# One bank for the natural scores and two for the Gram products in the second attention layer

## The reference

```python
scores_t = jnp.einsum('bhsd,bhtd->bhst', q, k_t) * attn_scale
probs_t = jax.nn.softmax(scores_t, axis=-1)
text_out = jnp.einsum('bhst,bhtd->bhsd', probs_t, v_t)
...
attn_scores = jnp.einsum('bhsd,bhnd->bhsn', q, k_ip) * attn_scale
qsem = jnp.einsum('bhst,bte->bhse', probs_t, text_ehs)
qsem = _l2norm(qsem)
ip_n = _l2norm(ip_ehs)
sem = jnp.einsum('bhse,bne->bhsn', qsem, ip_n)
fused = attn_scores + SEM_SCALE * sem
probs_ip = jax.nn.softmax(fused, axis=-1)
probs_ip = probs_ip * spatial_mask[None, None, :, None]
ip_out = jnp.einsum('bhsn,bhnd->bhsd', probs_ip, v_ip)
...
out = text_out + IP_SCALE * ip_out
out = out @ W_out + b_out
out = out + residual
```

## Time and profile before

| | us |
|---|---|
| median of 3 runs | 1635.77 |
| lowest, highest | 1634.82, 1635.92 |
| the profiled execution | 1634.38 |
| its span in the trace | 1632.3 |
| PE busy in the span | 1562.8 (96%) |
| DVE busy | 1393.3 (85%) |
| ACT busy | 1015.1 (62%) |
| POOL busy | 716.2 (44%) |

### The profile page before, as it was taken

One profiled execution on the slowest core, in us unless ns is written; L12 is line 12 of the kernel. 1 busy time (PEld: TensorE's weight loads), 2 busy tenths in 40 slices (PEclk: granted clock), 3 DMA queues, 4 the chain that ended last, 5 costly groups with the idle time before them and its releaser, 6 DMA issues.

```text
span 1632.3 us, 42423 instructions
## 1 busy us (share of the span) xinstructions
PE 1562.8 (96%) x13960; PEld 1385.0 (85%) x13960; DVE 1393.3 (85%) x4083; ACT 1015.1 (62%) x2444; POOL 716.2 (44%) x629
## 2 busy tenths in 40 slices
PE   6999999999999999998999999999999999999986
PEld 5888888888888888787798889988898888888965
DVE  4687787887888888876899999999999999999985
ACT  3455555565565566655667667667666777676652
POOL 3234432223322332433556555655655655555541
PEclk9999999999999999997999999999999999999988
DMA  8334444444444434543334323332333323332211
GB/s 228 99 107 122 121 126 131 119 127 125 123 130 124 124 117 128 142 124 97 90 91 123 101 69 109 104 105 70 106 95 105 95 83 104 108 103 65 82 38 35
DMA packets 204099, 175.29 MB, mean 107 GB/s; under 512 B 45313, under 2 KB 203403, under 8 KB 203883
## 3 DMA queue, kind: packets, MB, share of 16 engines
q1 hardware_dynamic: 203882, 172.59, 36.7%
HBM read 112.12 MB, written 60.38 MB: 106 GB/s over the span
## 4 chain that ended last, share of the span: by engine, by line
PE 87%; DVE 7%; issue 3%; ACT 1%; DMA 1%; SPq 1%; POOL 0%; DVEq 0%; ACTq 0%; POOLq 0%
PE MISC L144 26%; PE GP L144 20%; PE NAT L333 10%; PE TR L347 8%; PE PV L393 5%; PE PV L378 4%; PE PV L375 3%; PE PV L396 2%; PE MISC L293 2%; DVE ZP L957 1%; PE MISC L437 1%; DVE TMP L848 1%; PE MISC L436 1%; PE MISC L312 1%; PE GP L317 1%
## 5 line engine op out<-in xcount | busy, mean ns | idle before, releaser
L1050 POOL TENSOR_TENSOR ZS<-ZP 128x256 f32<-128x256 f32 x267 | 275.2, 1031 | 285.0 <-DVE ZP L957 284.0
L606 ACT ACTIVATE P<-TA 128x512 f32<-128x512 f32 x320 | 202.3, 632 | 279.3 <-DVE TA L945 276.1
L333 PE MATMUL NAT<-KS,QS 65*128 65x256 f32 x1280 | 300.0, 317 | 8.0 <-ACT SC L560 5.5
L967 DVE SCALAR_TENSOR_TENSOR PM<-P,PH 128x512 f32<-128x512 f32 x320 | 275.2, 860 | 0.0
L144 PE MATMUL GP<-PH,GH 128*128 128x256 f32 (+1 forms) x960 | 248.8, 289 | 21.4 <-DVE ZP L957 21.1
L347 PE MATMUL TR<-QS,KS 69*128 69x256 f32 (+2 forms) x1280 | 259.5, 284 | 4.1 <-DMA QS<-max_rows 2.2
L333 PEld LDWEIGHTS NAT<-KS,QS 65*128 65x128 f32 x1280 | 201.6, 192 | 64.4 <-issue 49.8
L852 DVE TENSOR_REDUCE MX<-NAT 128x2 f32<-128x504 f32 x320 | 215.9, 675 | 36.5 <-PE NAT L333 33.0
L144 PE MATMUL GP<-PH,GL 128*128 128x256 f32 (+1 forms) x960 | 242.7, 281 | 0.0
L281 POOL TENSOR_TENSOR PARTS<-QKF,PARTS 112x512 fp32r<-112x512 f32 (+1 forms) x93 | 121.2, 1304 | 276.0 <-ACT PARTS L635 233.4
L609 ACT ACTIVATE P<-TR 128x512 f32<-128x512 f32 x320 | 192.6, 602 | 60.1 <-PE TR L347 59.3
(11 more groups left out here) (264 smaller groups left out, 3784.6 us busy)
## 6 DMA issues: line engine op xcount, KB each, us to landing
QS<-qk_parts SPq DMA_DIRECT2D x480, 64.0 KB
KS<-qk_parts SPq DMA_DIRECT2D x480, 64.0 KB
qk_parts<-PARTS SPq DMA_DIRECT2D x128, 224.0 KB, 2.9
CT<-in_ctx_t SPq DMA_DIRECT2D x32, 512.0 KB, 3.9
qk_parts<-PARTS SPq DMA_DIRECT2D x64, 192.0 KB, 2.4
XT<-in_x_t SPq DMA_DIRECT2D x48, 112.0 KB, 2.7
XT<-x_t SPq DMA_DIRECT2D x48, 112.0 KB, 2.3
XB<-in_x SPq DMA_DIRECT2D x16, 320.0 KB, 4.2
```

Source lines behind the costliest of these rows:

```text
L333: ins = e.matmul(NAT[s % 2][:, i * T:(i + 1) * T], QS[0:KQ, h, i * 128:(i + 1) * 128], KS[0:KQ, h, :], start=True, stop=True)
L606: e.activation(P[:, s % NP, :], TA[:, s % 2, :], ACT.Exp, scale=SCALE).then_inc(q["exp"], 1)
L967: e.scalar_tensor_tensor(PM[:, s % 2, :], P[:, (S1 + s) % NP, :], 2.0, PH[:, s % NS, :].bitcast(F32), ALU.mult, ALU.subtract).then_inc(q[" ...
L1050: e.tensor_tensor(ZS[s % NZ][:, :], ZP[:, s % 2, 0:S], ZP[:, s % 2, S:2 * S], ALU.add).then_inc(q["zs"], 1)
```

## The change

Layer 1's natural scores all go to NAT[0]; NAT[1] becomes a second bank for the Gram products, which alternate between the old GP bank (even heads) and NAT[1] (odd heads). The waits follow: NAT waits for MX and SC of the head just before instead of two before, GP waits for ZP of two heads before instead of one (and head 1 for the last maximum of layer 0, which is the last reader of NAT[1]). PH gets one more wait, for PM of four heads before. Layer 0 keeps its two NAT banks. No instruction that computes is added or removed.

```diff
--- before.py
+++ after.py
@@ -221,7 +221,14 @@
     TR = [bank(f"TR{k}") for k in range(2)]
     PV = bank("PV")
     ring = Ring([bank(f"MISC{k}") for k in range(2)] + [bank("GP")])
-    GP = ring.banks[2]
+
+    def nat_bank(s):
+
+        return NAT[s % 2 if s < S1 else 0]
+
+    def gp_bank(s):
+
+        return (ring.banks[2], NAT[1])[s % 2]
 
     def take(key, freed, t, slots=None):
 
@@ -325,12 +332,14 @@
                     e.wait_ge(q["clear_q"], 1)
                 if h % HG == 0:
                     e.wait_ge(q[f"stack{h // HG}"], stacked(b + 1))
-                if s >= 2:
+                if s >= S1:
+                    e.wait_ge(q["mx"], s)
+                elif s >= 2:
                     e.wait_ge(q["mx"], s - 1)
-                if s >= S1 + 2:
-                    e.wait_ge(q["sc"], s - S1 - 1)
+                if s > S1:
+                    e.wait_ge(q["sc"], s - S1)
                 for i in range(2):
-                    ins = e.matmul(NAT[s % 2][:, i * T:(i + 1) * T], QS[0:KQ, h, i * 128:(i + 1) * 128],
+                    ins = e.matmul(nat_bank(s)[:, i * T:(i + 1) * T], QS[0:KQ, h, i * 128:(i + 1) * 128],
                                    KS[0:KQ, h, :], start=True, stop=True)
                 ins.then_inc(q["nat"], 1)
             s = t
@@ -356,11 +365,14 @@
                 if h == 0:
                     e.wait_ge(q["gl"], 3 * (b + 1))
                 e.wait_ge(q["ph"], s + 1)
-                if s:
-                    e.wait_ge(q["zp"], s)
+                if s == 1:
+                    e.wait_ge(q["mx"], S1)
+                if s >= 2:
+                    e.wait_ge(q["zp"], s - 1)
+                g = gp_bank(s)
                 p0, p1 = PH[:, k, 0:S], PH[0:N2, k, S:2 * S]
-                product(e, GP[:, 0:S], [(GH[:, p, 0, :], p0), (GL[:, p, 0, :], p0)])
-                product(e, GP[:, S:2 * S], [(GH[:, p, 1, :], p0), (GL[:, p, 1, :], p0), (GH[0:N2, p, 2, :], p1),
+                product(e, g[:, 0:S], [(GH[:, p, 0, :], p0), (GL[:, p, 0, :], p0)])
+                product(e, g[:, S:2 * S], [(GH[:, p, 1, :], p0), (GL[:, p, 1, :], p0), (GH[0:N2, p, 2, :], p1),
                                             (GL[0:N2, p, 2, :], p1)]).then_inc(q["gp"], 1)
             g = due_group(t, HG + 1, 0, G1)
             if g is not None:
@@ -557,7 +569,7 @@
                 if h == 0 and b >= 3:
                     e.wait_ge(q["fu"], 8 * (b - 3) + 2)
                 e.wait_ge(q["mx"], S1 + s + 1)
-                e.mul(SC[:, b % 3, :, NI * h:NI * h + NI], NAT[s % 2][:, :].rearrange("p (a t) -> p a t", a=2)[:, :, NT:T], SCALE).then_inc(q["sc"], 1)
+                e.mul(SC[:, b % 3, :, NI * h:NI * h + NI], nat_bank(S1 + s)[:, :].rearrange("p (a t) -> p a t", a=2)[:, :, NT:T], SCALE).then_inc(q["sc"], 1)
             g = due_group(t, HG + 4, 0, G1)
             if g is not None:
                 b, hg = divmod(g, NGRP)
@@ -609,6 +621,7 @@
                     e.activation(P[:, s % NP, :], TR[s % 2][:, :], ACT.Exp, scale=SCALE).then_inc(q["exp"], 1)
                     if s - S1 >= NS:
                         e.wait_ge(q["gp"], s - S1 - NS + 1)
+                        e.wait_ge(q["pm"], s - S1 - NS + 1)
                     e.wait_ge(q["exp"], s + 1)
                     e.copy(PH[:, s % NS, :], P[:, s % NP, :]).then_inc(q["ph"], 1)
             for off, lo, hi, width in ((HG + 1, 0, G1, 2 * S), (HG + 3, G1, 2 * G1, S)):
@@ -834,7 +847,7 @@
             if 0 <= s < 2 * S1:
                 b, h = divmod(s, H)
                 g, j, k = s // HG, h % HG, s % 2
-                v = NAT[k][:, :].rearrange("p (a t) -> p a t", a=2)
+                v = nat_bank(s)[:, :].rearrange("p (a t) -> p a t", a=2)
                 if j == 0 and g >= 2:
                     e.wait_ge(q["nh"], 2 * (g - 1))
                 if s >= 2:
@@ -954,7 +967,7 @@
                     e.wait_ge(q["zs"], s - 1)
                 e.wait_ge(q["pm"], s + 1)
                 e.wait_ge(q["gp"], s + 1)
-                e.tensor_tensor(ZP[:, s % 2, :], GP[:, :], PM[:, s % 2, :], ALU.mult).then_inc(q["zp"], 1)
+                e.tensor_tensor(ZP[:, s % 2, :], gp_bank(s)[:, :], PM[:, s % 2, :], ALU.mult).then_inc(q["zp"], 1)
             for n in range(ROOT_STEPS // 2):
                 b = at1(t, "rs", 1, n)
                 if b is not None:
```

## The result

The changed kernel takes 1888.2 us (median; 1886.1 to 1895.8) against 1635.3 of the kernel before: 1.157 times as long, 95% interval 1.155 to 1.159. The profiled execution took 1886.1 us, with a span of 1884.1; that is 251.8 us more than the span before.

What follows compares the result with a forecast made beforehand. PE was taken to set the pace, busy 98.47 of 100 us in layer two; NAT waiting for SC adds 15.6 us an element, 250 us over 16, so 1634.4+250+1.4=1886 us, range 1849 to 1970.

Steps and rivals of the forecast that it cites:

- the heads before element 0: Layer 1's ten heads ahead of the first batch element: taken at the steady rate of loss, 8 us.
- the sum: Steady part: 14.07 us lateness plus 1.80 way back less 0.25 Gram waits, 15.6 us per 20-slot element, 250 us over 16.
- the end: The last batch element's own schedule: taken to lose at the same rate as the steady elements.
- MX is no problem: NAT's new wait for MX of the head before: no cost, as MX is VectorE's first work in a slot.
- The lateness by kind of slot: SC's end less the next NAT load in the old trace: 14.07 us an element, over 15 of 20 slots.
- The way back from ScalarE to PE: From SC's end to the next NAT load: 0.12 us for each of fifteen waits, 1.80 us an element.
- The Gram bank: GP's relaxed wait for ZP: at most 21.1 us; beside the stalls 0.15 in slot 18 plus 0.1 elsewhere, 0.25 an element.
- PH's new wait for PM: PH on ScalarE also waits for VectorE's PM of four heads before: costed at nothing.
- rival 1: Each K slot's stall lowers PE's clock for a slot: 96 us more, 1982 us; half as many, 1934; chance 0.15.
- Rival 2: ScalarE lags only because permitted; NAT never waits and the second Gram bank gives back 21.1 us: 1615 us; chance 0.03.
- Rival 3: Waits removed and added are both hidden by PE's queue of other work: 1636 us; chance 0.03.
- Rival 4: Only the K slots and slot 17 stall, shorter evictions being overtaken by unseen work: 106 us, 1742 us; chance 0.06.

## Why the prediction was right

1886 us were forecast with a range from 1849 to 1970, and 1888.2 came. The mechanism is the one forecast; that the total came so close is in part luck. On the profiled spans 251.8 us came against 250: the heads before element 0 cost some 7 us more than their share of the sum and elements 1 and 2 some 9 more, while element 0 cost 0.5 less, elements 3 to 14 3.5 less and the end 10 less.

*What holds NAT.* SC and not MX, as the sum had it: PE's row shows SC 254 times, and the kernel with SC taken off the bank has no loss at all. Some 240 waits and 250 us were forecast, 254 and 229.9 are in PE's row. Its gaps are shorter than the stalls (in K slots 1.6 us where the slots grew by 1.8), as the ends of the products before them are modelled; the slots' lengths show the stalls whole. "MX is no problem" has one exception, in slot 17, which SC's longer lateness covers: there another piece of VectorE's work (HTL) stands before MX, and in the trace of before MX ends at 1228.03, 0.67 us behind the next load at 1227.36:

```profile
1227.36 0.67 DVE L852 TENSOR_REDUCE MX<-NAT 128x2 f32<-128x504 f32 x1
```

*The lateness by kind of slot.* The table above: of the 15 slots, 12 agree within 0.1 us and slot 15 within 0.11. Slot 13 was set 0.18 too long: before the change PE also stood still there, between GP and its own Gram products, probably until VectorE's GL had freed the MISC bank (the products' first load came 1.35 us after NAT's and 0.05 behind the end of GL, after the change 1.18), and the stall of slot 12 gives VectorE that time. Slot 14 was set 0.23 too short, having been given slot 16's smaller number; its own lateness in the trace of before, 0.92 us, would have given the 3.22 that came. The sum was 15.6 us an element; 15.3 came. The point on which all hung, that these latenesses count anew in each slot because the new wait lets ScalarE enter every slot empty, holds, and the kernel with SC behind PVS shows its reverse: where NAT isn't held until the K copies are done, slot 2 is late.

*The way back from ScalarE to PE.* 0.12 us from one place of the trace of before; 0.11 to 0.12 in the rows of after.

*The Gram bank.* Slot 18 was forecast at 3.32, slot 4 at 2.61; 3.24 and 2.59 came. PE's wait for ZP before GP went from 21.1 us to under 1. PH's new wait for PM, costed at nothing, ended none of ScalarE's waits in the trace of after. (The "last maximum of layer one" for which head 1's GP waits is that of layer 0, as in the change.)

*The heads before element 0* were one term that was mis-sized: 14.7 us in place of 8. I took them at the steady rate; ScalarE is there still at work on layer 0, and waits for VectorE between (PE's five waits for SC in the earlier trace rows averaged 1.1 us, not 0.8). In the trace of after, from 722 to 764 us:

```profile
ACT P L618 <- DVE TA L958: 18.7, 10, 2.4
...
PE NAT L342 <- ACT SC L572: 15.4, 10, 3.3
```

The granted clock of these heads is lower as well, 0.67 against 0.83 before. The kernel that keeps two NAT banks there, and does SC early, has all of the time back.

*The end*, which I took at the steady rate too (8 us), gave 2.0 us back instead. With one Gram bank it takes 88.6 us, 7.9 more than the 80.8 before, which is that rate; what the sum left out is that the second Gram bank makes it 9.8 us shorter (at a higher clock, as said above).

*The rivals.* The clock (rival 1) did fall, but not as that rival had it: in the steady part it is 1.00, K stalls of 1.75 us and all. In elements 0 to 2 it is 0.87 and 0.92. Elements 1 and 2 lost 40.1 us where the steady rate would be 30.6, and before the change their clock was 1.00. These 9.5 us lie with the falls: the slots of elements 1 and 2 that a fall touches take 9.2 us more than the same slots of elements 3 to 13, and all others together as long as those (medians). Slot 3 of element 2 and of element 5, with the clock behind the five engines:

```profile
921.40:927.32 5.92, 5.20 (x34) 3.20 (x35) 2.67 (x5) 1.67 (x4) 2.91 (x3) 0.50 0.30 90
...
1131.52:1135.12 3.60, 2.92 (x37) 1.96 (x35) 2.83 (x6) 1.67 (x4) 2.04 (x2) 1.00 0.44 129
```

That is 2.3 us more at the 1.2 GHz level, near the 2.0 at which rival 1 priced a slot, and the sum had put nothing on it. The four executions point the same way: 1886.1 and 1886.2 us at a mean clock of 0.970, 1890.2 at 0.968, 1895.8 at 0.964. Rival 2 (ScalarE could do SC in time if asked) fell with the time itself: 285 of layer 1's NAT loads stand 0.11 us behind the end of SC, which at its old place came no sooner than the evictions let it; in another place it did. Rival 3 fell with the changed kernel itself, and what stands behind it in the Trainium skill ("TensorE: Matmul & The Clock Gate", section "HAM oscillation — how this bites in real kernels": in a matmul kernel, double-buffering in PSUM gave no further gain) doesn't carry over to this kernel, where NAT's second bank, given up, cost 15.7%. Rival 4 fell with SC behind PVS.

*The shares.* Forecast 76, 74 and 54 in 100 for PE, VectorE and ScalarE between 1000 and 1100 us; 79.4, 68.5 and 55.5 came. VectorE's came out below the forecast for a reason of its own (last section).

Left open: why the clock fell in elements 0 to 2 and nowhere in elements 3 to 14.

## What to carry to other kernels

Before a bank is taken from a producer, look up its last reader, and ask what stands before that reader in its engine's queue: if it is work that waits for the same producer, the second bank was hiding that whole detour, however small the wait in the profile (5.5 us here; 229.9 after, and 253 us of time). The size can be read from the old trace, slot by slot, as the reader's end less the producer's next start. And the reader may be movable: here 0.18 us of ScalarE, put ahead of the evictions, made one bank nearly as good as two (1646.9 against 1634.6 us, with one Gram bank each). That alone was no gain; with the other bank used for the Gram products, and kept for NAT in the first 12 heads, the kernel is 0.7% faster than before.

## What else the runs showed of the hardware

VectorE's PM takes 0.68 us in most heads, but in the kernel before some took 2 us. Line L967 of before, minimum, median and maximum in ns:

```profile
L967 DVE SCALAR_TENSOR_TENSOR PM<-P,PH x320: 669/681/2266, 753.5 to 1606.4; 128x512 f32<-128x512 f32 x160
```

The same instruction in the changed kernel, L980:

```profile
L980 DVE SCALAR_TENSOR_TENSOR PM<-P,PH x320: 674/681/1272, 768.2 to 1858.1; 128x512 f32<-128x512 f32 x160
```

One slow PM in the timeline of before, with what POOL did beside it:

```profile
1187.96 2.06 DVE L967 SCALAR_TENSOR_TENSOR PM<-P,PH 128x512 f32<-128x512 f32 x1
...
1187.48 1.30 POOL L281 TENSOR_TENSOR PARTS<-QKF,PARTS 112x512 fp32r<-112x512 f32 x1 [0.53 <-ACT PARTS L641]
...
1188.73 0.73 POOL L1050 TENSOR_TENSOR ZS<-ZP 128x256 f32<-128x256 f32 x1
```

The same place in the timeline of after:

```profile
1199.49 0.68 DVE L980 SCALAR_TENSOR_TENSOR PM<-P,PH 128x512 f32<-128x512 f32 x1
...
1197.18 1.29 POOL L288 TENSOR_TENSOR PARTS<-QKF,PARTS 112x512 fp32r<-112x512 f32 x1 [0.53 <-ACT PARTS L654]
...
1199.72 1.05 POOL L1063 TENSOR_TENSOR ZS<-ZP 128x256 f32<-128x256 f32 x1 [1.25 <-DVE ZP L970]
```

PM reads two tensors from SBUF. All 30 PMs of before that started while POOL's PARTS was running ended 0.55 us behind the end of POOL's next ZS. Of the 320 PMs of before, 46 took over 1.4 times the median, 58 us too long in sum; 30 of them are these, and 14 started beside the context's low half (CTSL) and ended 0.55 us behind it. After, none started beside PARTS, and two took over 1.4 times the median. The Trainium skill, "SBUF — State Buffer", section "SBUF: two separate sides", has VectorE instructions with two SBUF inputs and GpSimd instructions that read SBUF share a port pair that the first one holds to its end. The rows agree, and they show that the blocked time is counted as busy; that POOL's next ZS also went ahead of the waiting PM, the section doesn't say. In the changed kernel the stalls moved PM off those places, and its busy time fell from 275.2 to 221.8 us, which gained nothing, as VectorE wasn't what PE waited for. Whether these 58 us would help a kernel in which VectorE is late was not tried.
